# A convolution layer on one core: weight sums and the first image's additions given to transfers

## The chip, the cores and the metric

The kernel runs on one core of one Trainium2 chip. The metric is device time in microseconds (us), the median over several executions. Before the change it is 1605.91 us (three runs, 1605.81 to 1606.45).

## The reference

The input x has 32 images of 256 channels and 28 x 28 points, in float32. Twelve fixed masks (two radius levels, six angle bins, 9 x 9 points) average each channel around each point; a strided 4 x 3 convolution mixes the twelve averages and the 256 channels into 256 channels, and a 1 x 1 convolution of x itself is added. Then comes batch normalization over all images with the batch's own mean and variance, then x is added and negative values are cut off:

```python
xp  = log_pooling(x)                                  # 12 averages of each channel
out = conv(xp, w_conv1, stride (4, 3)) + conv(x, w_center) + b_center
mean, var = out.mean(axis=(0, 2, 3)), out.var(axis=(0, 2, 3))
out = (out - mean) * rsqrt(var + 1e-5) * gamma + beta
return relu(out + x)
```

## The kernel before, in words

The 256 channels stand as 128 partitions times 2 halves (`c` counts input halves, `o` output halves). A step `s` is one input half of one image (s = 2 * image + c); there are 64. In a step VectorE (DVE) makes differences and sums of the columns of x (`differences`), running sums over three and four rows (`three_columns`, `boxes`), and from them three pairs of pooled planes (`first_sum`, `second_sum`, `third_sum`). TensorE (PE) has the first image's products and every other's in the same order: the "middle" products on D1 and D2 (into banks 4 to 7), then the "inner" ones on VD and SD, then the three pairs j = 0, 1, 2 of pooled planes (all into banks 0 to 3).

Each product is made three times, in float32r: the data and the weights are split into a high part (a copy rounded by ScalarE, ACT: lines 397, 400, 418 for data, 392 for weights) and a low part (value minus high part, on DVE: `lo_of_sums`, `lo_of_shifted`, `lo_of_pooled`, and `lo_of_weights`, L557). High x high, low x high and high x low are lines 772 to 774.

The weights are prepared in the first image only, for each input half. `transform_weights` (L523) makes six 256-column combinations of the raw weights on DVE, five instructions at L533 to L543; `split_weights` (L382) and `lo_of_weights` (L547) then split seven groups: group 0 (1536 columns, the combinations, factor 1/4), groups 1 to 4 (256 columns each) and the two outer groups 5 and 6 (512 and 1024 columns). PE waits for group 0 before the middle products, for groups 0 to 4 before the inner ones, and for group 5 and 6 before pairs 0 and 1.

When an image's products have ended, its result is assembled in `y_stage`: ACT copies the middle banks there (`copy_middle`, L433), DVE makes sum and difference of its even and odd columns (`take_middle`, L568 and L571) and adds banks 0 to 3 (`take_y`, L579). ACT then sums it and its squares (`measure`, L451), after finding in the first image a pivot for each channel (`make_pivot`, L442). SyncE (SP) saves y to DRAM (L321). PE may write a bank of the next image only when these readers are done (`m_copied`, `y_ready`).

GpSimd (POOL) issues two adding transfers in each step (L270): `row2` and `ends` get the padded x added from DRAM onto what ACT has put there (`row2_begun`, `ends_begun`). `wait_first` is a wait and a semaphore step on POOL ahead of each. SP loads x and the raw weights; the second part of the first half's weights, the second half of x and all weights of the second half are issued after the first `row2` transfer has landed, in this order. All instructions of an engine's queue run in the order of the program. PE begins with 70 products of zeros (L779), and the tail after the last image reads y and x again, scales, adds, cuts and stores.

The program's own text names the order of the first image (`first_image`, L677) and of every other (`image_steps`, L696). Two lines say what the change turns on:

```python
dve.wait_ge(w_hi_ready, c * len(GROUPS) + g + 1)     # L550, the low part waits for the high one
dve.wait_ge(middle_taken, image + 1 + FREE)          # L576, banks 0-3 are added after the middle
```

Of the kernel before, what the change touches and what calls it, by code (L numbers as in the profile page):

```python
# [7 lines left out]
def conv_bn_relu_program(nc, x, x_wide, w_raw, b_center, gamma, beta, out, y_dram):  # L8
# [62 lines left out]
    with ctx:  # L71
# [61 lines left out]

        def w_part(c, lo, tap):

            if tap < INNER_TAPS:
                return (w_first, w_inner)[c], (lo * INNER_TAPS + tap) * CHANNELS
            return (w_first_outer, w_outer)[c], (lo * (TAPS - INNER_TAPS) + tap - INNER_TAPS) * CHANNELS

# [59 lines left out]
        w_loaded = [[sem(f"w_loaded{c}{part}") for part in range(2)] for c in range(CH)]  # L199
        w_sums_ready = sem("w_sums_ready")  # L200
        w_moved = sem("w_moved")
        w_hi_ready = sem("w_hi_ready")
        w_lo_ready = sem("w_lo_ready")
        zeroed = sem("zeroed")
# [21 lines left out]
        m_copied = sem("m_copied")  # L226
        middle_summed = sem("middle_summed")
# [28 lines left out]
        ZEROED = 7  # L256

        @block.gpsimd
        def _(pool):
            n = 0  # L260
            for edge in (std[:, :], pooled_split[:, 2 * PAIR:2 * PAIR + HALF], row2[:, :], ends[:, :],
                         x_pad[:, 0:2 * H], x_pad[:, X_PAD:X_PAD + 2 * H], x_pad[:, CH * X_PAD:]):
# [26 lines left out]
            with pool.Fori(1, IMAGES) as image:  # L289
                image_sums(image)  # L290
# [9 lines left out]
        def _(sp):  # L300
# [49 lines left out]
            sp.wait_ge(w_lo_ready, CH * len(GROUPS))  # L350
# [30 lines left out]
        def _(act):  # L381
            def split_weights(c, groups):  # L382
                for g in groups:
                    a, b, raw, factor = GROUPS[g]
                    if raw is None:
                        act.wait_ge(w_sums_ready, c + 1)
                        source = view(y_stage, 0, (1, (b - a) * CHANNELS))
# [4 lines left out]
                    nc.scalar.activation(view(dst, at, (1, (b - a) * CHANNELS)), source, ACT.Copy,  # L392
                                         scale=factor).then_inc(w_hi_ready, 1)

# [27 lines left out]
            def copy_middle(image):  # L422
# [7 lines left out]
                if isinstance(image, int) and image == 0:  # L430
                    act.wait_ge(w_lo_ready, CH * len(GROUPS))
# [4 lines left out]

            def make_pivot():

                for o in range(CH):
                    act.wait_ge(y_ready, o + 1 + FREE)  # L440
# [15 lines left out]
            def image_steps(image, first=False, second=False, last=False):  # L456
                for c in range(CH):
                    s = CH * image + c
                    if c == 0 and not first:
                        copy_middle(image - 1)  # L460
                    split_inner(s)
                    if c == 1 and not first:
                        measure(image - 1, 1)
                    if first:
                        split_weights(c, range(len(GROUPS)))
                        act.wait_ge(warmed_up, 1)
                    following = (image, 1) if c == 0 else (image + 1, 0)
# [10 lines left out]
                    if second and c == 0:  # L478
                        make_pivot()
                    if c == 0 and not first:  # L480
# [32 lines left out]
        def _(dve):  # L513
# [9 lines left out]
            def transform_weights(c):  # L523
# [8 lines left out]
                wait_from_one(dve, w_lo_ready, len(GROUPS) * c)  # L532
# [5 lines left out]
                dve.wait_ge(w_moved, 2 * c + 1)  # L538
# [3 lines left out]
                dve.wait_ge(w_moved, 2 * c + 2)  # L542
# [4 lines left out]
            def lo_of_weights(c, groups):  # L547
                for g in groups:
                    a, b, raw, factor = GROUPS[g]
                    dve.wait_ge(w_hi_ready, c * len(GROUPS) + g + 1)  # L550
                    if raw is None:
                        source = view(y_stage, 0, (1, (b - a) * CHANNELS))
# [57 lines left out]
            def differences(image, c):  # L610
# [4 lines left out]
                nc.vector.memset(view(d03, 0, (TALL, 2 * U), (TALL - 1, 2)), 0.0)  # L615
# [23 lines left out]
            def three_columns(image, c):  # L639
# [5 lines left out]
                nc.vector.memset(row3v(-ROW3V_AT, (ROW3V_H, W + 3), (1, EDGES)), 0.0)  # L645
# [31 lines left out]
            def first_image():  # L677

                for c in range(CH):
# [9 lines left out]
                    lo_of_weights(c, [FIRST_OUTER_GROUP - 1])  # L689
# [6 lines left out]
            def image_steps(image, second=False):  # L696
                for c in range(CH):
# [3 lines left out]
                    if c == 0:  # L701
                        take_middle(image - 1)
                    else:
                        lo_of_pooled(s - 1, PAIRS - 1)
# [3 lines left out]
                    if second and c == 0:  # L708
                        take_y(image - 1)
# [12 lines left out]
            dve.sem_inc(middle_taken, FREE)  # L722
# [42 lines left out]
        def _(pe):  # L765
# [17 lines left out]
            with pe.Fori(0, IMAGES) as image:  # L783
                for c in range(CH):
# [29 lines left out]
                    for j in range(PAIRS):  # L814
                        pe.wait_ge(w_lo_ready, c * len(GROUPS) + min(FIRST_OUTER_GROUP + j, len(GROUPS)))
# [55 lines left out]
```

## Time and profile before

| | |
|---|---|
| median of three runs | 1605.91 us (1605.81 to 1606.45) |
| the profiled execution, its own time | 1605.88 us |
| its span, first to last instruction | 1604.1 us |
| PE busy | 1458.2 us (91%) |
| DVE busy | 1474.4 us (92%) |
| ACT busy | 760.6 us (47%) |
| POOL busy | 122.6 us (8%) |
| transfers | 197.55 MB, 123 GB/s over the span |
| mean granted TensorE clock | 0.958 |

Busy shares are averages over the span. The profile's chain of waits gives 86% of the span to PE. A time "idle before" names the engine that ended an engine's idle stretch; a row's start plus its duration is its end, though neighbouring DVE and ACT rows overlap by about 0.1 us, so distances are best taken from start to start.

### The profile page before, as it was taken

To read this page: it belongs to the slowest core of one execution; us is meant where nothing else is said; L and a number is where in the kernel's file an instruction comes from. 1 tells how busy PE (TensorE), PEld (TensorE's weight loads), DVE (VectorE), ACT (ScalarE), POOL (GpSimd) and SP (SyncE) were. 2 spreads that over 40 slices of the span, in tenths; PEclk is the share of its full clock that TensorE was granted. 3 is DMA by queue.
4 is the path that set the end of the run, shared out by engine and by line. 5 is a ranking of instruction groups with operands and counts; after the bars stand their busy time and mean duration, and the time that the engine had idled before them with its cause. 6 is when DMAs were issued, how large, how long until landed. Compare 5 with 4: busy or idle time off the path is not lost.

```text
span 1604.1 us, 22797 instructions
## 1 busy us (share of the span) xinstructions
PE 1458.2 (91%) x8518; PEld 1456.1 (91%) x8518; DVE 1474.4 (92%) x1512; ACT 760.6 (47%) x853; POOL 122.6 (8%) x155
## 2 busy tenths in 40 slices
PE   9899999999999999999999999999999999995000
PEld 9899999999999999999999999999999999995000
DVE  8999999999999999999999999999999999996731
ACT  4345555445444554445444554445444554444632
POOL 1000000000000000000000000000000000000100
PEclk9999999999999999999999999999999999998555
DMA  6244443344333443344333443344334444569999
GB/s 170 69 80 88 84 94 81 80 94 84 81 80 74 85 93 81 80 94 84 81 80 74 87 92 82 80 94 84 83 79 77 87 89 103 155 198 380 419 425 398
DMA packets 46632, 197.55 MB, mean 123 GB/s; under 512 B 5536, under 2 KB 5536, under 8 KB 46624
## 3 DMA queue, kind: packets, MB, share of 16 engines
q0 software_dynamic: 20736, 82.45, 28.4%
q1 hardware_dynamic: 21024, 89.32, 15.2%
q10 hardware_dynamic: 4864, 25.69, 3.9%
q8 instruction: 2, 0.03, 0.0%
q14 instruction: 6, 0.05, 0.0%
HBM read 147.67 MB, written 49.77 MB: 123 GB/s over the span
## 4 chain that ended last, share of the span: by engine, by line
PE 86%; DVE 4%; ACT 4%; ACTq 3%; issue 1%; DMA 0%; DVEq 0%
PE acc L772 29%; PE acc L774 29%; PE acc L773 29%; ACTq L509 3%; ACT phase L506 2%; ACT phase_rest L506 2%; DVE phase_rest L514 1%; DVE pooled_split L515 1%; DVE d L514 0%; DVE inner_split L515 0%; DVE y_stage L514 0%; ACT unread L451 0%; ACT x_pad L506 0%; DMA x_pad<-x 0%; ACT w_inner L392 0%
## 5 line engine op out<-in xcount | busy, mean ns | idle before, releaser
L418 ACT ACTIVATE pooled_split<-phase_rest 128x1456 fp32r<-128x1456 f32 x192 | 273.0, 1422 | 595.5 <-DVE phase_rest L514 595.5
L515 DVE TENSOR_TENSOR pooled_split<-phase_rest,pooled_split 128x1456 fp32r<-128x1456 f32 x192 | 317.8, 1669 | 0.0
L772 PE MATMUL acc<-pooled_split,w_first_outer 128*128 128x364 f32 x768 | 253.8, 330 | 1.1 <-DVE pooled_split L515 1.1
L772 PE MATMUL acc<-pooled_split,w_outer 128*128 128x364 f32 x768 | 252.2, 328 | 1.5 <-DVE pooled_split L515 1.4
L774 PE MATMUL acc<-pooled_split,w_outer 128*128 128x364 f32 x768 | 252.7, 329 | 0.0
L773 PE MATMUL acc<-pooled_split,w_first_outer 128*128 128x364 f32 x768 | 252.5, 329 | 0.0
L773 PE MATMUL acc<-pooled_split,w_outer 128*128 128x364 f32 x768 | 252.5, 329 | 0.0
L774 PE MATMUL acc<-pooled_split,w_first_outer 128*128 128x364 f32 x768 | 252.3, 328 | 0.0
L772 PE MATMUL acc<-inner_split,w_inner 128*128 128x392 f32 (+1 forms) x640 | 215.8, 337 | 2.9 <-DVE w_inner L557 2.9
L772 PE MATMUL acc<-inner_split,w_first 128*128 128x392 f32 (+1 forms) x640 | 216.8, 339 | 0.2 <-DVE inner_split L515 0.2
L773 PE MATMUL acc<-inner_split,w_inner 128*128 128x392 f32 (+1 forms) x640 | 216.6, 338 | 0.0
L774 PE MATMUL acc<-inner_split,w_inner 128*128 128x392 f32 (+1 forms) x640 | 216.6, 338 | 0.0
L774 PE MATMUL acc<-inner_split,w_first 128*128 128x392 f32 (+1 forms) x640 | 215.9, 337 | 0.0
L773 PE MATMUL acc<-inner_split,w_first 128*128 128x392 f32 (+1 forms) x640 | 215.5, 337 | 0.0
L397 ACT ACTIVATE inner_split<-phase_rest 128x1568 fp32r<-128x1568 f32 x64 | 97.2, 1519 | 128.1 <-DVE phase_rest L514 128.1
L772 PEld LDWEIGHTS acc<-pooled_split,w_outer 128*128 128x128 f32 x768 | 144.2, 188 | 2.1 <-DVE pooled_split L515 2.1
L772 PEld LDWEIGHTS acc<-pooled_split,w_first_outer 128*128 128x128 f32 x768 | 144.4, 188 | 1.7 <-DVE pooled_split L515 1.4
L773 PEld LDWEIGHTS acc<-pooled_split,w_outer 128*128 128x128 f32 x768 | 144.5, 188 | 0.0
L773 PEld LDWEIGHTS acc<-pooled_split,w_first_outer 128*128 128x128 f32 x768 | 144.5, 188 | 0.0
L774 PEld LDWEIGHTS acc<-pooled_split,w_outer 128*128 128x128 f32 x768 | 144.4, 188 | 0.0
L774 PEld LDWEIGHTS acc<-pooled_split,w_first_outer 128*128 128x128 f32 x768 | 144.4, 188 | 0.0
L270 POOL DMA_DIRECT2D row<-x_wide x64 | 55.6, 869 | 1093.2 <-ACT row L407 1077.5
(95 smaller groups left out, 2486.1 us busy)
## 6 DMA issues: line engine op xcount, KB each, us to landing
row<-x_wide POOLq DMA_DIRECT2D x64, 558.0 KB, 5.8
ends<-x_wide POOLq DMA_DIRECT2D x64, 504.0 KB, 5.5
x_pad<-x SPq DMA_DIRECT2D x64, 392.0 KB, 3.1
y_dram<-y_stage SPq DMA_DIRECT2D x30, 784.0 KB, 3.3
out<-phase ACTq DMA_DIRECT2D x16, 784.0 KB, 28.4
phase<-y_dram SPq DMA_DIRECT2D x15, 784.0 KB, 16.7
phase_rest<-y_dram SPq DMA_DIRECT2D x14, 784.0 KB, 14.1
out<-phase_rest ACTq DMA_DIRECT2D x14, 784.0 KB, 30.0
```

The costliest lines, as they stand in the source:

```text
L270: return pool.dma_start(view(buf, 0, (1, n_columns * TALL_PITCH)), x_wide[bass.ds(image, 1), :, c, bass.ds((first_column + EDGE) * TALL_PI ...
L397: nc.scalar.activation(view(inner_split, 0, (1, SD)), reused_view(INNER_LOW, (1, SD)), ACT.Copy)\
L418: nc.scalar.activation(view(pooled_split, 2 * j * PAIR, (1, PAIR)), reused_view(POOLED_LOW + 2 * j * PAIR, (1, PAIR)), ACT.Copy)\
L506: nc.scalar.activation(x_slot(d, o), x_slot(d, o), ACT.Relu, bias=bn_shift[:, o:o + 1]).then_inc(relu_done, 1)
L509: act.dma_start(out[tail_image(round_, d)].rearrange("p c w h -> p c (w h)"), x_slot_whole(d)).then_inc(stored[d], 16)
L514: add = lambda out_, a, b: nc.vector.tensor_tensor(out_, a, b, ALU.add)
L515: sub = lambda out_, a, b: nc.vector.tensor_tensor(out_, a, b, ALU.subtract)
L772: nc.tensor.matmul(place, hi_w, hi_in, start=start, stop=False)
L773: nc.tensor.matmul(place, lo_w, hi_in, start=False, stop=False)
L774: return nc.tensor.matmul(place, hi_w, lo_in, start=False, stop=stop)
```

## The change

For the second input half (c = 1) the six weight combinations are no longer made by five DVE instructions. POOL issues a chain of five transfers of 384 KB (128 partitions x 768 columns), one plain and four adding, each waiting until the one before has landed; the three outer terms come from a new array `w_side` laid out on the host by rearranging the raw weights, the middle term is added twice. One DVE instruction makes the other three combinations from the result. The chain stands in POOL's queue between the two transfers of step 0 and those of step 1.

The two outer groups of c = 1 are split without DVE: ACT writes the high part, the scaled weights, and the negated high part in the place of the low one; POOL then adds the scaled weights onto it by a transfer within the core's memory (256 KB and 512 KB). These stand in POOL's queue behind the transfers of step 1.

For image 0, ACT copies the middle banks to `spare` in two forms (as they are, and spread to the other column with sign +1 and -1), later copies banks 0 to 3 straight into `y_stage`, and POOL adds the two forms by two transfers of 784 KB, one after the other, behind the transfers of step 2. DVE has no `take_middle` and no `take_y` for image 0. SP waits for both additions ahead of the steps of image 1, and ACT ahead of the pivot, which moves behind `split_inner` of step 3. Two small memsets of step 0 move from DVE to POOL's opening, and `ZEROED` counts them.

```diff
@@ POOL
                     add_from(image, c, ends, 2, W).then_inc(ends_ready, 16)
+                    if isinstance(image, int) and image == 0:
+                        (sum_weights, low_outer_weights)[c]()
+                    if isinstance(image, int) and image == 1 and c == 0:
+                        add_first_middle()
+            def sum_weights():
+                parts = [w_side[:, k, :] for k in range(3)]
+                parts += 2 * [w_raw[:, 1, RAW_MID:RAW_MID + 3, :].rearrange("p k o -> p (k o)")]
+                pool.dma_start(w_sums(1, 0, 3), parts[0]).then_inc(w_plus_ready, 16)
+                for k in range(1, len(parts)):
+                    wait_first(w_plus_ready, 16 * k)
+                    pool.dma_start(w_sums(1, 0, 3), parts[k], accum_op=ALU.add).then_inc(w_plus_ready, 16)
+            def low_outer_weights():
+                for g in range(INNER_GROUPS, len(GROUPS)):
+                    high, low, whole = outer_weights(g)
+                    wait_first(w_outer_begun, g - INNER_GROUPS + 1)
+                    pool.dma_start(low.bitcast(F32), whole, accum_op=ALU.add).then_inc(w_outer_lo_ready[g - INNER_GROUPS], 16)
+            def add_first_middle():
+                wait_first(y_ready, CH + FREE)
+                wait_first(first_spread, 1)
+                for m in range(2):
+                    if m > 0:
+                        wait_first(first_added, 16 * m)
+                    pool.dma_start(y_stage[:, :], first_middle(m, 0, (1, CH * HW)), accum_op=ALU.add)\
+                        .then_inc(first_added, 16)
@@ SP
             image_steps(0, first=True)
+            sp.wait_ge(first_added, 32)
@@ ACT
+            def begin_outer_weights(g):
+                act.wait_ge(w_loaded[1][1], 16)
+                nc.scalar.activation(high, source, ACT.Copy, scale=factor).then_inc(w_outer_hi_ready, 1)
+                nc.scalar.activation(whole, source, ACT.Copy, scale=factor)
+                act.wait_ge(w_outer_hi_ready, g - INNER_GROUPS + 1)
+                nc.scalar.activation(low, high.bitcast(F32), ACT.Copy, scale=-1.0).then_inc(w_outer_begun, 1)
+            def take_first():
+                for m in range(2):
+                    act.wait_ge(m_copied, m + 1 + FREE)
+                    spread = nc.scalar.activation(first_middle(m, H, ...), first_middle(m, 0, ...), ACT.Copy,
+                                                  scale=(1.0, -1.0)[m])
+                spread.then_inc(first_spread, 1)
+                act.wait_ge(w_lo_ready, ALL_LO)
+                act.wait_ge(pooled_done, PAIRS * CH)
+                for o in range(CH):
+                    nc.scalar.activation(view(y_stage, o * HW, ...), view(acc, 2 * o * BANK, ...), ACT.Copy)\
+                        .then_inc(y_ready, 1)
             def make_pivot():
+                act.wait_ge(first_added, 32)
@@ ACT image_steps
+                    if c == 0 and second:
+                        copy_first_middle()
+                    if first and c == 1:
+                        begin_outer_weights(INNER_GROUPS)
                     split_inner(s)
+                    if c == 0 and second:
+                        take_first()
+                    if c == 1 and second:
+                        make_pivot()
+                        measure(image - 1, 0)
...
+                        split_weights(c, range(len(GROUPS) if c == 0 else INNER_GROUPS))
                         act.wait_ge(warmed_up, 1)
+                    if first and c == 1:
+                        begin_outer_weights(INNER_GROUPS + 1)
@@ DVE transform_weights
+                if c == 1:
+                    dve.wait_ge(w_plus_ready, 5 * 16)
+                    nc.vector.scalar_tensor_tensor(out=w_sums(1, 3, 3), in0=raw(RAW_MID, 3), scalar=-4.0,
+                                                   in1=w_sums(1, 0, 3), op0=ALU.mult, op1=ALU.add)\
+                        .then_inc(w_sums_ready, 1)
+                    return
@@ DVE first_image and image_steps
-                    lo_of_weights(c, range(FIRST_OUTER_GROUP, len(GROUPS)))
+                    if c == 0:
+                        lo_of_weights(c, range(FIRST_OUTER_GROUP, len(GROUPS)))
...
-                    if second and c == 0:
-                        take_y(image - 1)
@@ PE
+                        if c == 0:
+                            pe.wait_ge(w_lo_ready, min(FIRST_OUTER_GROUP + j, len(GROUPS)))
+                        elif j < 2:
+                            pe.wait_ge(w_outer_lo_ready[j], 16)
```

## Rows read from the trace of the kernel before

**Rows 1.** Busy time by stretch: start:end, length, engines' busy us, PEclk, DMA share, GB/s.

```profile
20.00:80.00 60.00, 54.32 (x311) 52.63 (x310) 59.62 (x64) 25.49 (x26) 4.29 (x5) 1.00 0.32 72
80.00:1450.00 1370.00, 1370.00 (x8028) 1369.84 (x8027) 1329.18 (x1342) 662.22 (x739) 104.84 (x121) 1.00 0.42 91
```

**Rows 2.** Timeline of PE, products that began after a wait: start, us, instruction, [idle before].

```profile
41.62 0.44 PE L772 MATMUL acc<-inner_split,w_inner 128*128 128x392 f32 x1 [2.94 <-DVE w_inner L557]
...
53.81 0.43 PE L772 MATMUL acc<-pooled_split,w_outer 128*128 128x364 f32 x1 [1.38 <-DVE pooled_split L515]
...
66.61 0.44 PE L772 MATMUL acc<-inner_split,w_first 128*128 128x392 f32 x1 [0.20 <-DVE inner_split L515]
...
78.49 0.43 PE L772 MATMUL acc<-pooled_split,w_first_outer 128*128 128x364 f32 x1 [1.07 <-DVE pooled_split L515]
```

**Rows 3.** Timeline of DVE, first image, second half.

```profile
37.16 0.96 DVE L543 SCALAR_TENSOR_TENSOR y_stage<-w_stage,y_stage 128x768 f32<-128x768 f32 x1
38.03 1.78 DVE L515 TENSOR_TENSOR inner_split<-phase_rest,inner_split 128x1568 fp32r<-128x1568 f32 x1
39.73 1.75 DVE L557 SCALAR_TENSOR_TENSOR w_inner<-y_stage,w_inner 128x1536 fp32r<-128x1536 f32 x1
...
51.48 0.69 DVE L557 SCALAR_TENSOR_TENSOR w_outer<-w_stage,w_outer 128x512 fp32r<-128x512 f32 x1
...
55.32 1.22 DVE L557 SCALAR_TENSOR_TENSOR w_outer<-w_stage,w_outer 128x1024 fp32r<-128x1024 f32 x1
```

**Rows 4.** Timeline of DVE, second image.

```profile
64.69 1.79 DVE L515 TENSOR_TENSOR inner_split<-phase_rest,inner_split 128x1568 fp32r<-128x1568 f32 x1
...
69.54 1.85 DVE L514 TENSOR_TENSOR y_stage<-acc,y_stage 128x784 f32<-128x784 f32 x2
...
90.69 0.97 DVE L514 TENSOR_TENSOR d<-row,x_pad 128x840 f32<-128x840 f32 x1
```

**Rows 5.** Timeline of ACT.

```profile
29.00 0.85 ACT L407 ACTIVATE ends<-x_pad 128x784 f32<-128x784 f32 x1
35.16 1.52 ACT L397 ACTIVATE inner_split<-phase_rest 128x1568 fp32r<-128x1568 f32 x1 [5.31 <-DVE phase_rest L514]
...
38.15 1.49 ACT L392 ACTIVATE w_inner<-y_stage 128x1536 fp32r<-128x1536 f32 x1 [0.72 <-DVE y_stage L543]
...
62.92 1.53 ACT L397 ACTIVATE inner_split<-phase_rest 128x1568 fp32r<-128x1568 f32 x1 [3.89 <-DVE phase_rest L514]
```

**Rows 6.** Timeline of POOL, the issue of adding transfers.

```profile
6.35 1.23 POOL L270 DMA_DIRECT2D ends<-x_wide  x1
...
30.42 0.86 POOL L270 DMA_DIRECT2D ends<-x_wide  x1 [4.22 <-ACT ends L407]
```

**Rows 7.** Transfers, KB each, us from issue to landing: 0:12, 12:40 (two rows), 1404:1420.

```profile
ends<-x_wide POOLq DMA_DIRECT2D x1, 504.0 KB, 7.7
...
row<-x_wide POOLq DMA_DIRECT2D x1, 558.0 KB, 5.8
ends<-x_wide POOLq DMA_DIRECT2D x1, 504.0 KB, 5.4
...
ends<-x_wide POOLq DMA_DIRECT2D x1, 504.0 KB, 9.6
```

**Rows 8.** Busy time by stretch, as rows 1: while the raw weights load, and after.

```profile
16.00:18.00 2.00, 2.00 (x13) 2.00 (x12) 1.97 (x4) 1.55 (x2) 0.00 (x0) 1.00 1.04 434
...
22.00:24.00 2.00, 2.00 (x13) 2.00 (x13) 2.00 (x3) 1.59 (x2) 0.00 (x0) 1.00 0.03 13
```

**Rows 9.** Busy time by stretch, as rows 1: the granted clock at both ends.

```profile
2.00:4.00 2.00, 2.00 (x8) 2.00 (x7) 0.00 (x0) 0.43 (x2) 1.42 (x5) 1.00 0.97 344
...
1465.00:1466.00 1.00, 0.31 (x2) 0.01 (x1) 0.65 (x1) 0.00 (x0) 0.00 (x0) 1.00 1.02 427
...
1469.00:1470.00 1.00, 0.00 (x0) 0.00 (x0) 0.00 (x0) 0.97 (x3) 0.00 (x0) 1.00 1.00 420
1470.00:1471.00 1.00, 0.00 (x0) 0.00 (x0) 0.27 (x1) 0.70 (x2) 0.00 (x0) 0.54 1.05 439
```

More of the change, by code:

```diff
@@ L138, in w_part, with w_sums, outer_weights, first_middle @@
             return (w_first_outer, w_outer)[c], (lo * (TAPS - INNER_TAPS) + tap - INNER_TAPS) * CHANNELS
+        def w_sums(c, first, n):
+            return view((y_stage, spare)[c], first * CHANNELS, (1, n * CHANNELS))
+        ALL_LO = len(GROUPS) + INNER_GROUPS
+        def outer_weights(g):
+            a, b = (t - INNER_TAPS for t in GROUPS[g][:2])
+            n = (1, (b - a) * CHANNELS)
+            return (view(w_outer, a * CHANNELS, n),
+                    view(w_outer, (TAPS - INNER_TAPS + a) * CHANNELS, n),
+                    view(spare, (6 + a) * CHANNELS, n))
+        def first_middle(m, first, *dims):
+            return view(spare, 12 * CHANNELS + m * CH * HW + first, *dims)
         LAST = IMAGES - 1
@@ L203, in conv_bn_relu_program @@
         w_lo_ready = sem("w_lo_ready")
+        w_outer_hi_ready = sem("w_outer_hi_ready")
+        w_outer_begun = sem("w_outer_begun")
+        w_outer_lo_ready = [sem(f"w_outer_lo_ready{k}") for k in range(2)]
         zeroed = sem("zeroed")
@@ L286, in image_sums @@
                     add_from(image, c, ends, 2, W).then_inc(ends_ready, 16)
+                    if isinstance(image, int) and image == 0:
[22 more added lines that the diff above has]
+                        .then_inc(first_added, 16)
             image_sums(0)
-            with pool.Fori(1, IMAGES) as image:
+            image_sums(1)
+            with pool.Fori(2, IMAGES) as image:
                 image_sums(image)
@@ L349, in _ @@
             image_steps(LAST - 2)
-            sp.wait_ge(w_lo_ready, CH * len(GROUPS))
+            sp.wait_ge(w_lo_ready, ALL_LO)
+            for k in range(2):
+                sp.wait_ge(w_outer_lo_ready[k], 16)
             sp.wait_ge(y_saved, 16 * (LAST - 3))
@@ L458, in image_steps @@
                     s = CH * image + c
-                    if c == 0 and not first:
+                    if c == 0 and second:
+                        copy_first_middle()
+                    elif c == 0 and not first:
                         copy_middle(image - 1)
+                    if first and c == 1:
+                        begin_outer_weights(INNER_GROUPS)
                     split_inner(s)
+                    if c == 0 and second:
[3 more added lines that the diff above has]
+                        measure(image - 1, 0)
                     if c == 1 and not first:
@@ L477, in image_steps @@
                         begin_ends(*following)
-                    if second and c == 0:
-                        make_pivot()
-                    if c == 0 and not first:
+                    if c == 0 and not first and not second:
                         measure(image - 1, 0)
@@ L614, in differences @@
                 wait_from_one(dve, pooled_ready, PAIRS * s)
-                nc.vector.memset(view(d03, 0, (TALL, 2 * U), (TALL - 1, 2)), 0.0)
+                if not (isinstance(image, int) and s == 0):
+                    nc.vector.memset(d_edges(), 0.0)
                 sub(view(d03, 1, (U * TALL, 2), (TALL, U), (1, H)),
@@ L644, in three_columns @@
                 wait_from_one(dve, pooled_done, PAIRS * s - PAIRS + 1)
-                nc.vector.memset(row3v(-ROW3V_AT, (ROW3V_H, W + 3), (1, EDGES)), 0.0)
+                if not (isinstance(image, int) and s == 0):
+                    nc.vector.memset(row3v_edges(), 0.0)
                 dve.wait_ge(inner_lo_ready, 2 * s + 2)
@@ L699, in image_steps @@
                     differences(image, c)
-                    if c == 0:
+                    if c == 1:
+                        lo_of_pooled(s - 1, PAIRS - 1)
+                    elif not second:
                         take_middle(image - 1)
-                    else:
-                        lo_of_pooled(s - 1, PAIRS - 1)
                     lo_of_sums(s)
@@ L845 @@
     w_raw = np.ascontiguousarray(w[:, order][:, :, by_half].reshape(128, halves, len(order), channels))
+    a, c, d, f = (w_raw[:, 1, k] for k in range(4))
+    w_side = np.stack([np.concatenate(part, axis=1) for part in ((d, d, a), (f, a, c), (f, np.zeros_like(a), c))], axis=1)
     def per_partition(v):
```

48 lines of the change are left out of this document (32 added, 16 removed).

## The prediction

> **What bounds the kernel now.** I read the busy time by stretch first, to see which engine is never idle and when. From 80 to 1450 us PE is busy for all 1370 us while DVE has 41 us to spare; from 20 to 80 us it is the other way round, DVE 59.6 of 60 us and PE 54.3 [rows 1]. So after 80 us nothing can be won off PE, and the start is where DVE work holds PE up. The timeline of PE shows the four places: PE had ended at 38.68 and began the second half's products at 41.62; it waited again before 53.81, 66.61 and 78.49, each time for a low part from DVE [rows 2]. The waits sum to 2.94 + 1.38 + 0.20 + 1.07 = 5.6 us. That is the most a change of this start can give. After 78.49 PE runs through to its end, and the tail behind it is released by PE's last products, so what the start gains or loses there is carried to the end unchanged, unless something later holds PE up anew. I therefore follow one number, PE's start of pair 0 of the second image, 78.49 before.
>
> **The chain for the weight sums.** This sets the result, since DVE now stands in its queue before `lo_of_sums(1)` until five transfers have landed. Before, the last instruction of the sums began at 37.16 and PE began 4.46 us later: 0.87 to the low part of the data, 1.70 to the low part of the weights (1536 columns), 1.75 for that and 0.14 to PE [rows 2, 3]; ACT's high part of the sums, 38.15 to 39.64, fits in exactly [rows 5]. The new kernel's one instruction for c = 1 is of the same kind, 768 columns and 0.96 us, and has the same followers. Call its start T. PE begins the second half at 41.62 + (T - 37.16).
>
> T is the landing of the fifth transfer. When does it land?
>
> The first, plain one is issued at 7.6 us, when POOL has ended the issue of `ends` (6.35 + 1.23) [rows 6], but lies in the same queue behind `ends`, which landed at 6.35 + 7.7 = 14.05 [rows 6, 7]. At 434 GB/s its 384 KB need 0.9 us; it shares the engines with SP's loads, which keep them full [rows 8]. I take 2.9 us (bounds 1 and 5): 16.9.
>
> Each of the next four waits for the landing and is then issued. ACT's `ends` copy ended at 29.85 and POOL's issue began at 30.42 [rows 5, 6]: 0.57 us, taken for each. The adding transfers that ran alone took 5.8 us for 558 KB and 5.4 for 504 [rows 7]. Continued to 384 KB by that difference it is 4.5; the upper bound is 5.4 itself; I take 4.65. One beside a deep queue of loads took 9.6 us for 504 KB [rows 7]. The second transfer meets such a queue: SP's loads ended at 22 us [rows 8], will end about 1 us later with the plain one between them, and the second is issued at 17.5. It is neither alone nor beside loads all the way; I take 7.7 us (bounds 4.6 and 9.6), landing 25.2. The three others run alone: 3 x (0.57 + 4.65) = 15.7. T = 40.9. With all low bounds T is 35.3, with all high ones (19, 29.2, then 3 x 5.97) it is 47.
>
> The Trainium skill has a rule that speaks for this edit: its page "DMA: Bandwidth & Descriptors", section "Anatomy of one DMA — SWDGE (gpsimd) path", fits such a transfer at 2.0 us plus its bytes at 436 GB/s, an estimate of 2.9 us for 384 KB. By that rule the chain would be over near 31 us and nobody would wait. This trace disagrees for adding ones: the rule would give 3.3 us for the 558 KB that took 5.8. I go by the row.
>
> So PE begins at 41.62 + 3.74 = 45.4 and stands idle for 6.7 us where it was 2.94.
>
> **The outer groups.** Two DVE instructions go: 0.69 us before pair 0's low part and 1.22 before pair 1's [rows 3], which less the overlap of neighbouring rows is 0.60 and 1.14. ACT makes six copies of 512 or 1024 columns instead; it has room, as it sat idle for 5.31 us before 35.16 [rows 5]. The two transfers are issued behind the chain, `row2` and `ends` of step 1, at about 39 and 48 us, and land by 47 and 54; PE needs them at 57 and 61. Cover about 7 us; nothing. `row2` itself, issued at 25 before, comes at about 37.5 and lands near 44, while DVE, itself 3.7 us late, asks at 47.6. Nothing, but this cover shrinks if T grows no further with it: both sit on the same chain.
>
> **Pair 0, second half.** Its low part is late by 3.74 - 0.60 = 3.1: PE could begin at 56.95. PE's inner products end at 52.43 + 3.74 = 56.2 at full clock. Still a wait of 0.8 us.
>
> **The first image's result.** `take_middle` leaves DVE, but the low part that followed it at 64.69 also needed ACT's high part, which ended at 64.45 [rows 4, 5]: of the 1.9 us removed only 0.24 count. `take_y` before the boxes is 1.85 us [rows 4], 1.77 less the overlap, and counts fully on DVE. By then DVE is late by 3.74 - 0.60 - 1.14 - 0.24 - 1.77 = 0 and its low part of pair 0 is ready at 78.4, as before; PE gets there later than that. So the waits before 66.61 and 78.49 go. PE at full clock: 56.95 + 12.60 (53.81 to 66.41, pairs of image 0) + 10.81 (66.61 to 77.42) = 80.4 against 78.49: +1.9 us. In general this is T - 39.0.
>
> **The clock.** After PE's last product at 1465.3 the granted clock was still 1.00 from 1469 to 1470 and fell within the next microsecond, to half (1.2 GHz), 4.8 us after the work had stopped [rows 9]. The idle stretch of 2.94 us did not bring it down (1.00 over that stretch) [rows 1]. One of 6.7 us will. What it costs: at the start of the program PE's products went 8 in 2 us from 2 to 4 us and 13 later at 2.4 GHz [rows 8, 9]; the lower rate lasted from 1.4 us to nearly 6, some 4.4 us of work, so about 2.2 us are lost (bounds 1 and 3.4). The wait of 0.8 us before pair 0 swallows part: +1.4.
>
> **The two additions to y.** PE ends image 0 at 56.95 + 12.60 + 1.4 = 70.9; ACT copies banks 0 to 3 in some 1.9 us, the time of DVE's two adds from there [rows 4], so the first is issued at 73.4. For 784 KB I continue the rows to 7.4 us each (bounds 6.5 and 8.2 by proportion, twice that if a transfer within the core is slower): landings at 80.8 and 88.8. Queued behind on POOL is `row2` of step 3, which lands near 92.7; DVE used it at 90.69 [rows 4], so DVE is 2.0 us late there. PE's need is later: its first pooled product of that step comes at 78.49 + 12.0 (the three pairs) + 10.8 + 3.3 = 104.6, DVE's low part, about 9 us after the `row2` add (an estimate: in the second image's first half it is the 78.4 less some 67.5 less 1.8), at 101.7. Cover 3 us. ACT waits for the second addition until 88.8, then has six passes over 784 columns for pivot and sums, each about the 0.85 us of its `ends` copy [rows 5] and a short read-out, some 6.2 us; it is free at 95.0 and wanted at about 98. SP's wait delays load and save to 89; the loaded x is wanted past 98. All at nothing; if an addition takes over 1.5 us more than I say, PE pays twice the excess.
>
> The two memsets, of 56 and 124 columns, leave DVE in the first half of image 0, where PE does not wait for DVE: nothing.
>
> **Sum.** +1.9 + 1.4 = +3.3 us. The profiled execution took 1605.88 us, the median 1605.91: 1609.2.
>
> **Rivals.**
> Forecast, chance 0.55: chain late by 3 to 5 us and the clock falls, 1607.5 to 1611.5.
> (B) The chain is late but T is 38 to 40 and the stall, at most 5.8 us, falls between the 2.94 that kept the clock and the 4.8 that lost it, or just over: 1605.91 + (39.2 - 39.0) = 1606.1. For it: the plain transfer and the second may be nearer their low bounds. Against: four adding transfers at over 5 us. Chance 0.22.
> (C) No wait for the chain: it decides if T is under 36.3. Then ACT sets the pace: inner splits 35.16 to 37.4, sums' high part to 38.9, PE at 40.8, pair 0 at 53.81 - 0.8 - 0.6 = 52.4, then 12.60 + 10.81: 75.8, -2.7 us, 1603.2. It needs links of 3.6 us, under every adding transfer in the rows, or a chain unhurt by loads. Chance 0.10. (It is also what follows from the rule of the Trainium skill quoted above.)
> (D) The additions to y come late: a rate within the core half of that from DRAM makes both 14 us, `row2` of step 3 lands 13 us later and PE loses 10 us of it on top: 1619; at a quarter more, 1611. Nothing in the trace shows such a transfer; chance 0.08. The rest, 0.05, is the unforeseen.
>
> **How the numbers follow.** A measurement here tells 0.2% (3.2 us: 1602.7 and 1609.1) from no change. My forecast lies on the upper bound, so its 0.55 is 0.30 slower and 0.25 within; B is 0.19 within and 0.03 slower (the clock falls after all); C 0.07 within and 0.03 faster; D slower; the rest 0.03 slower, 0.02 faster. Together: faster 0.05, within 0.51, slower 0.44. The range takes in B and half of what lies between B and C below, and above a T of 44 with the clock down: 1604.0 to 1612.5.
>
> **What would show it.** PE's wait before the second half's first product: 6.7 us, ended by DVE `w_inner`; DVE idle before its 768-column sum, until 40.9, by a transfer; landings of the chain 5.2 us apart; the granted clock at half for some 4 us from 43 to 50; no wait before 66 and 78. It is wrong if PE's wait is under 4 us, if the clock stays at 1.00, or if PE waits at all between 80 and 110.

## The result, and the profile after

The changed kernel takes 1609.01 us (median of 20 runs, 1607.51 to 1609.81) against 1606.42 us for the kernel before in the same runs (20, 1605.67 to 1607.27): ratio 1.0015, 95% interval 1.0009 to 1.0021, so 2.6 us slower, against a forecast of 1609.2 (3.3 us slower). The profiled execution took 1608.33 us, its span is 1606.6 us.

PE now waits once where it waited four times [rows 2]. The timeline of PE after the change, from 20 to 110 us, has one row with an idle time; the second row here is pair 0 of the second image, the number the prediction followed:

```profile
46.68 0.69 PE L884 MATMUL acc<-inner_split,w_inner 128*128 128x392 f32 x1 [7.77 <-DVE w_inner L665]
...
81.57 0.33 PE L884 MATMUL acc<-pooled_split,w_first_outer 128*128 128x364 f32 x1
```

That pair began at 78.49 before: 3.1 us later. PE's last product is 2.95 us later (1467.94 against 1464.99), the span 2.5. So all of the difference is made before 82 us and carried through.

DVE stands idle ahead of its one sum instruction, and its followers come at the old distances [rows 3]:

```profile
42.21 0.96 DVE L637 SCALAR_TENSOR_TENSOR spare<-w_stage,spare 128x768 f32<-128x768 f32 x1 [6.84 <-DMA spare<-w_raw]
43.09 1.78 DVE L617 TENSOR_TENSOR inner_split<-phase_rest,inner_split 128x1568 fp32r<-128x1568 f32 x1
44.79 1.75 DVE L665 SCALAR_TENSOR_TENSOR w_inner<-spare,w_inner 128x1536 fp32r<-128x1536 f32 x1
```

The chain itself, by POOL's timeline. Each row's start is an issue; the idle time is the wait for the landing before it:

```profile
7.11 1.25 POOL L326 DMA_DIRECT2D spare<-w_side  x1
15.99 0.86 POOL L329 DMA_DIRECT2D spare<-w_side  x1 [7.63 <-DMA spare<-w_side]
25.62 0.86 POOL L329 DMA_DIRECT2D spare<-w_side  x1 [8.77 <-DMA spare<-w_side]
31.19 0.86 POOL L329 DMA_DIRECT2D spare<-w_raw  x1 [4.71 <-DMA spare<-w_side]
37.07 0.86 POOL L329 DMA_DIRECT2D spare<-w_raw  x1 [5.01 <-DMA spare<-w_raw]
```

And the same transfers by their time from issue to landing, asked for one at a time, the first to the fifth:

```profile
spare<-w_side POOLq DMA_DIRECT2D x1, 384.0 KB, 8.3
...
spare<-w_side POOLq DMA_DIRECT2D x1, 384.0 KB, 9.1
...
spare<-w_side POOLq DMA_DIRECT2D x1, 384.0 KB, 5.0
...
spare<-w_raw POOLq DMA_DIRECT2D x1, 384.0 KB, 5.3
...
spare<-w_raw POOLq DMA_DIRECT2D x1, 384.0 KB, 5.1
```

The second ran beside SP's loads, the last three almost alone. A landing and the next issue are 0.5 to 0.6 us apart (15.99 + 9.1 = 25.1, then 25.62).

The granted clock, by stretch (PEclk is the column before the last two): half for the whole stretch in which PE resumed, and full right after.

```profile
46.68:50.46 3.78, 3.78 (x12) 3.78 (x13) 3.75 (x9) 2.08 (x3) 0.87 (x1) 0.50 0.45 83
50.50:52.00 1.50, 1.50 (x11) 1.50 (x9) 1.47 (x2) 0.00 (x0) 0.00 (x0) 1.00 0.99 180
```

By the starts in PE's timeline the products follow each other at 0.32 us at half the clock (49.39, 49.71) and at 0.17 to 0.18 at the full one (51.11, 51.28, 51.46); the 11 of the second row count two products that began before the stretch too.

### The profile page after: what moved, and what is told of

It reads as the page before. It is cut to its first block, busy times and chain, and to the rows that moved or that the text cites. A ratio compares the mean times of both kernels' runs of the same rounds, so it can differ in the third digit from the quotient of the medians.

```text
span 1606.6 us, 22801 instructions
## 1 busy us (share of the span) xinstructions
PE 1459.1 (91%) x8518; PEld 1458.3 (91%) x8518; DVE 1467.5 (91%) x1500; ACT 767.3 (48%) x861; POOL 130.4 (8%) x166
## 4 chain that ended last, share of the span: by engine, by line
PE 88%; ACT 4%; ACTq 3%; DMA 2%; DVE 1%; issue 0%; POOL 0%; POOLq 0%; DVEq 0%
PE acc L884 30%; PE acc L886 29%; PE acc L885 29%; ACTq L611 3%; ACT phase L608 2%; ACT phase_rest L608 2%; DMA spare<-w_side 1%; DMA spare<-w_raw 1%; ACT unread L544 0%; ACT x_pad L608 0%; DMA x_pad<-x 0%; DVE inner_split L617 0%; DVE w_inner L665 0%; DVE y_stage L616 0%; DVE spare L637 0%
```

## The experiments

The profiled programs are named here by what they do; "lost" and "gained" are against the kernel before in the same runs.

**The weight sums back on DVE.**

```diff
-                        (sum_weights, low_outer_weights)[c]()
+                        if c == 1:
+                            low_outer_weights()
...
-                if c == 1:
-                    dve.wait_ge(w_plus_ready, 5 * 16)
...   (the five DVE instructions serve c = 1 again, in spare)
```

> The change without the chain: the second half's weight sums are made by five DVE instructions again, the outer groups and the first image's result stay with transfers. Theory 1 (the chain of five transfers is all of the loss, the other edits gain): PE's wait before the second half falls from 7.77 to about 3 us, the granted clock stays at 1.00, pair 0 of the second image begins near 76.8 instead of 81.57, and the time is 1604.3 us, some 2 us under the kernel before. Theory 2 (the transfers for the outer groups or for y cost as well, by their place in POOL's queue): PE waits somewhere between 50 and 110 us and the time is 1606.5 or more.

Measured: 1604.2 us (before 1606.23; ratio 0.9988, 95% interval 0.9979 to 0.9997; the later results are written the same way). One wait of 2.96 us on PE, pair 0 of the second image at 76.42. Without the chain the change is a gain of 2 us; theory 2 falls. Against expectation the clock did fall, for a wait of the old length, and the wait before pair 0 of the first image was gone. PE arrived later there; in the second execution of this program, below, where the clock stayed up, the wait is back.

**The chain alone**, put into the kernel before.

```diff
                     add_from(image, c, ends, 2, W).then_inc(ends_ready, 16)
+                    if isinstance(image, int) and image == 0 and c == 0:
+                        sum_weights()
...   (transform_weights, w_sums and w_side as in the change)
```

> The kernel before with the chain of five transfers alone. Theory 1: PE's wait is 7.8 us as in the changed kernel, and what DVE no longer gives back (1.74 us of outer groups, 1.9 and 1.77 us of the first image's result) shows as a wait of about 1 us before pair 0 of the second image, which begins at 83.5: 1611.2 us, 4.8 over the kernel before. Theory 2: the chain costs less than that alone, since two of its causes add up only in the changed kernel: 1608 to 1609.

Measured: 1610.65 us (1.0027, 1.0016 to 1.0038), 4.4 lost. PE waits 7.05 and then, as theory 1 has it, before pair 0 of the second image:

```profile
83.05 0.43 PE L794 MATMUL acc<-pooled_split,w_first_outer 128*128 128x364 f32 x1 [1.08 <-DVE pooled_split L531]
```

The interval (1608.8 to 1612.3 us) holds the times of both theories; the wait of 1.08 us before pair 0 is what separates them, and it is there.

**One link fewer, one link more.** Both programs compute wrong weights for the second half: one leaves out an addition of the middle term, the other makes one too many.

```diff
-                parts += 2 * [w_raw[:, 1, RAW_MID:RAW_MID + 3, :].rearrange("p k o -> p (k o)")]
+                parts += 1 * [w_raw[:, 1, RAW_MID:RAW_MID + 3, :].rearrange("p k o -> p (k o)")]   # 3 * in the other
...
-                    dve.wait_ge(w_plus_ready, 5 * 16)
+                    dve.wait_ge(w_plus_ready, 4 * 16)                                              # 6 * 16
```

> The changed kernel with one transfer fewer in the chain (the second addition of the middle term is left out, so the weights of the second half are not the right ones; the work is the same otherwise). Theory 1 (the end of the chain sets PE's start, one for one, and the clock falls only for the long wait): the chain lands at 36.6, PE begins at 41.1 after 2.2 us, clock 1.00, a wait of 0.7 us before pair 0 of the first image: 1603.5 us, 5.5 less than the changed kernel, of which 4.7 are the link and the rest the clock and what hides. Theory 2 (the clock has no part in it): 5.6 - 0.8, so 1604.3 us.

> The changed kernel with one more transfer in the chain (the middle term added a third time, so the weights of the second half are not the right ones). Theory 1: the chain lands at 47.8, PE waits 13.4 us, and as the clock is down already in the changed kernel the step is the link alone, 5.6 us: 1614.6 us. Theory 2 (POOL's queue behind the chain decides too: row2 of step 1 lands near 52.8, DVE wants it at 54.6): nothing more; if it does, over 1616.

Measured: four links 1602.8 us (0.9979, 0.9970 to 0.9988), six links 1615.47 (1.0053, 1.0040 to 1.0067). PE's waits for the second half's weights, four links and then six:

```profile
40.97 0.44 PE L884 MATMUL acc<-inner_split,w_inner 128*128 128x392 f32 x1 [1.89 <-DVE w_inner L665]
52.55 0.43 PE L884 MATMUL acc<-pooled_split,w_outer 128*128 128x364 f32 x1 [0.75 <-DVE pooled_split L617]
```

```profile
51.54 0.69 PE L884 MATMUL acc<-inner_split,w_inner 128*128 128x392 f32 x1 [12.57 <-DVE w_inner L665]
```

Four, five and six links give 1602.8, 1609.0 and 1615.5: 6.2 and 6.5 us a link, where PE's start moved by 5.7 and 4.9. From five to six the end of the chain and PE's start move one for one. From four to five they do not quite: with four links DVE's sum instruction began at 35.83, 6.4 us sooner than with five, and PE's start came 5.14 us behind it instead of 4.47, since the low part of the weights now waited 0.33 us for ACT. At four links the chain has just stopped deciding, and ACT sets the pace, as rival C has it for a T under 36.3:

```profile
35.83 0.96 DVE L637 SCALAR_TENSOR_TENSOR spare<-w_stage,spare 128x768 f32<-128x768 f32 x1 [0.46 <-DMA spare<-w_raw]
```

That the clock has a part is shown by the traces (1.00 throughout with four links, half for 3.8 us of work with five), not by the time: the 1604.3 us of theory 2 lies on the upper bound of the interval for four links. Pair 0 of the second image began at 75.13, 81.57 and 87.53. For six links I had argued that the clock's price was paid already. It was not: the clock was down for 6.2 us of work there, against 3.8.

**The clock held up** by 40 products of zeros while PE waits, and its partner without them. POOL writes the zeros behind the plain transfer of the chain, and ACT waits for the 40 products before it overwrites them with the second outer group.

```diff
-            with pe.Fori(0, IMAGES) as image:
+            def image_products(image):
...
+                    if isinstance(image, int) and image == 0 and c == 1:
+                        pe.wait_ge(idle_zeros, 1)
+                        held = w_outer[:, 2 * CHANNELS:2 * CHANNELS + HALF]
+                        for k in range(40):
+                            idle = nc.tensor.matmul(view(acc, 7 * BANK, (1, HALF)), held[:, 0:P], held, start=False, stop=False)
+                        idle.then_inc(idle_done, 1)
...
+            image_products(0)
+            with pe.Fori(1, IMAGES) as image:
+                image_products(image)
```

> The changed kernel with 40 products of zeros (they add nothing) on PE while it waits for the second half's weights, so that the clock has no idle stretch to fall in; PE's first image stands outside the loop for it. Theory 1 (the fall of the clock took 1.9 us of PE's work, but a wait for pair 0's low part, ready at 58.2, takes its place for the first 1.1 us): PE begins the second half at 46.7 as before, clock 1.00, inner products end at 57.5, a wait of 0.7 us, pair 0 of the second image near 80.9: 0.7 to 0.8 us less than the same kernel without them. Theory 2 (the clock is worth all it took): 1.9 us less. Theory 3 (it is worth nothing, as what is recorded as half is not on the path): the same time.

> The changed kernel with PE's first image outside the loop and no products of zeros, the partner of the run before. Both theories: as the changed kernel, 1609 us, 2.6 over the kernel before, a wait of 7.8 us and a clock that falls to half. If it differs by over 0.5 us, taking the first image out of the loop has a price of its own.

Measured: held 1609.22 us (1.0019, 1.0010 to 1.0028), partner 1609.79 (1.0022, 1.0013 to 1.0031). The mean granted clock of a whole execution was 0.957 to 0.959 in all eleven with the zeros and 0.954 or 0.955 in all eleven without, which speaks for the zeros having held it each time. The medians differ by 0.6 as theory 1 says, but the intervals overlap, so the times alone do not settle it. The timelines, one execution each, say more. With the clock held PE starts the second half at 46.36 at full clock and then waits:

```profile
40.00:46.00 6.00, 6.00 (x35) 5.88 (x34) 4.02 (x3) 2.72 (x5) 0.33 (x1) 1.00 1.03 196
...
46.36 0.45 PE L889 MATMUL acc<-inner_split,w_inner 128*128 128x392 f32 x1 [0.16 <-DVE w_inner L670]
...
58.11 0.40 PE L889 MATMUL acc<-pooled_split,w_outer 128*128 128x364 f32 x1 [0.93 <-DVE pooled_split L622]
...
80.65 0.33 PE L889 MATMUL acc<-pooled_split,w_first_outer 128*128 128x364 f32 x1
```

What the clock takes can be read from the stretch between the start of the second half and pair 0 of the first image. Without its wait the held run needs 10.82 us for it (11.75 - 0.93):

| run | the stretch, us | waiting in it | at half clock | over 10.82: the clock's price |
|---|---|---|---|---|
| clock held | 11.75 | 0.93 | 0 | |
| partner | 12.22 | 0 | 3.4 | 1.40 |
| changed kernel | 12.39 | 0 | 3.8 | 1.57 |
| loads held back (below) | 13.41 | 0 | 6.1 | 2.59 |

So 0.41 to 0.43 of the time at half clock is lost, less than a half, and 0.93 us of that would have been waiting anyway. For the partner that leaves 0.47, and its pair 0 of the second image is indeed 0.43 us later, counted from its own start (34.72 us from 46.17 to 80.89, against 34.29). So in these traces theory 2 falls, and theory 3 too.

The partner was meant to equal the changed kernel. It was 3.4 us over the kernel before where the changed kernel is 2.6, and by what I had set down beforehand a difference of over 0.5 means that taking the first image out of the loop has a price of its own. The intervals overlap, and in its profile pair 0 of the second image and PE's last product come 0.7 us sooner than in the changed kernel; what makes that execution longer lies behind PE's last product. Such a price is neither shown nor excluded, and the held run is compared with its partner alone.

**A chain of three links**, for the outer terms only.

```diff
-                parts += 2 * [w_raw[:, 1, RAW_MID:RAW_MID + 3, :].rearrange("p k o -> p (k o)")]
...
+                    dve.wait_ge(w_plus_ready, 3 * 16)
+                    nc.vector.scalar_tensor_tensor(out=w_sums(1, 3, 3), in0=raw(RAW_MID, 3), scalar=-2.0,
+                                                   in1=w_sums(1, 0, 3), op0=ALU.mult, op1=ALU.add)
+                    nc.vector.scalar_tensor_tensor(out=w_sums(1, 0, 3), in0=raw(RAW_MID, 3), scalar=2.0,
+                                                   in1=w_sums(1, 0, 3), op0=ALU.mult, op1=ALU.add)\
+                        .then_inc(w_sums_ready, 1)
```

> A complete kernel: the change with a chain of three transfers, for the outer terms only; DVE adds twice the middle term and its negative in two instructions instead of one. Theory 1 (the chain costs nothing when it lands before DVE comes for it at 35.3): it lands at 30.7, DVE's second instruction begins at 36.3, ACT's splits set the pace, PE begins the second half at 41.0 after 2.1 us, waits 0.7 before pair 0 and nowhere else: 1602.9 us, 3.4 under the kernel before and as fast as four links. Theory 2 (the transfers cost something by being there, beside the loads): 1604 or more, no better than the change without the chain.

Measured: 1603.13 us (before 1606.38; 0.9979, 0.9970 to 0.9988), 3.3 under the kernel before, and it computes the whole reference. It has the lowest median of the complete kernels here, though its interval overlaps with that of the plain transfer first (1603.53), below. PE's waits:

```profile
40.84 0.44 PE L885 MATMUL acc<-inner_split,w_inner 128*128 128x392 f32 x1 [1.52 <-DVE w_inner L666]
52.42 0.43 PE L885 MATMUL acc<-pooled_split,w_outer 128*128 128x364 f32 x1 [0.74 <-DVE pooled_split L616]
```

PE's start and waits are those of theory 1 (41.0, 2.1 and 0.7); by the time alone the 1604 of theory 2 lies within the interval. DVE's first sum instruction began at 35.15 with no wait for the chain, so a chain over before it is wanted costs nothing that shows.

**The first image's result alone.**

```diff
...   (weight sums as in the first experiment, and also)
-                    if c == 0:
-                        lo_of_weights(c, range(FIRST_OUTER_GROUP, len(GROUPS)))
+                    lo_of_weights(c, range(FIRST_OUTER_GROUP, len(GROUPS)))
...
-                    if first and c == 1:
-                        begin_outer_weights(INNER_GROUPS)
```

> Of the change only the first image's result by ACT and two transfers (and the two memsets); the second half's weight sums and outer groups on DVE as before. Theory 1: the waits of 2.94 and 1.38 us stay, those of 0.20 and 1.07 go: 1605.0 us, 1.3 under the kernel before; the outer groups are then worth the 0.8 us that are left to the run without the chain. Theory 2 (the outer groups gain nothing, their 1.74 us of DVE are cover): 1604.2 us like that run.

Measured: 1604.78 us (0.9988, 0.9979 to 0.9997), a gain of 1.6. The interval holds the times of both theories, the waits decide: those of 2.93 and 1.37 us stay, no other is left, and pair 0 of the second image begins at 77.23. The outer groups add 0.4 to 0.6 us by the medians, within the intervals; in the profiles, 0.8 (76.42), but the clock had fallen in that execution. Against the other execution of that program, with the clock up as here (last experiment, pair 0 at 75.86), it is 1.4 us: 0.6 of it the shorter wait before pair 0 of the first image.

**Loads held back** until the second transfer has landed.

```diff
+            sp.wait_ge(w_plus_ready, 2 * 16)
             load_weights(1, 0)
             load_weights(1, 1)
```

> The changed kernel, but SP issues the two loads of the second half's weights only when the second transfer of the chain has landed. In the changed kernel that second transfer took 9.1 us where the later ones took 5.0 to 5.6. Theory 1 (an adding transfer beside these loads takes about 8 us, whichever it is): the second takes 5.3 us and lands at 21.3, the third 8, the chain lands at 41.5, and the time is 1608.5 us, at most 0.8 under the changed kernel. Theory 2 (what costs is a load queue already deep when the transfer is issued, and one that fills later costs little): the third takes 5.5, the chain lands at 38.9, PE waits 4.5 us: 1605.5 us.

Measured: 1608.75 us (1.0015, 1.0006 to 1.0024). The second and the third transfer, by the time from issue to landing:

```profile
spare<-w_side POOLq DMA_DIRECT2D x1, 384.0 KB, 5.4
...
spare<-w_side POOLq DMA_DIRECT2D x1, 384.0 KB, 8.2
```

Theory 1: the dear transfer is the one beside the loads, whichever it is. The sum instruction began at 41.41, 0.8 sooner; the longer time at half clock (45.87 to 51.93) ate that in the profiled execution.

**The plain transfer first.**

```diff
             assert n == ZEROED
+            pool.dma_start(w_sums(1, 0, 3), w_side[:, 0, :]).then_inc(w_plus_ready, 16)
...
-                pool.dma_start(w_sums(1, 0, 3), parts[0]).then_inc(w_plus_ready, 16)
```

> The changed kernel with the first, plain transfer of the chain issued right behind POOL's memsets, ahead of the two transfers of step 0, instead of behind them; a complete kernel. Theory 1 (the chain's end is its start plus its links): it lands near 8, the second is issued behind ends of step 0 and lands at 17.5, the third meets the loads and takes 9, landing at 27, the chain at 38.3, four less than in the changed kernel; PE waits 4 us and the clock stays up in most executions: 1605.0 us. Theory 2 (the loads of x and of the first weights, which it now meets, are on the path): they land 1 us later, the first products come later than 15.9 and half of it is lost again: 1606.5.

Measured: 1603.53 us (0.9983, 0.9974 to 0.9992), 5.5 less than the changed kernel for one line moved. POOL's timeline, then PE's only wait from 20 to 110 us, then the stretch behind it:

```profile
3.57 0.68 POOL L298 DMA_DIRECT2D spare<-w_side  x1
...
7.75 0.86 POOL L329 DMA_DIRECT2D spare<-w_side  x1 [0.26 <-issue]
16.77 0.85 POOL L329 DMA_DIRECT2D spare<-w_side  x1 [8.16 <-DMA spare<-w_side]
26.30 0.86 POOL L329 DMA_DIRECT2D spare<-w_raw  x1 [8.69 <-DMA spare<-w_side]
...
41.78 0.69 PE L884 MATMUL acc<-inner_split,w_inner 128*128 128x392 f32 x1 [2.32 <-DVE w_inner L665]
...
41.78:45.12 3.34, 3.34 (x10) 3.34 (x11) 3.31 (x9) 2.08 (x3) 0.67 (x1) 0.50 0.50 92
```

The sum instruction began at 37.32, 4.9 sooner. Its first product came at 16.75 in the profiled execution, later than 16.05 in the changed kernel; at the start PE's products reached the full rate about 2 us later in it (between 7 and 9 us, not 5 and 7), so I do not charge the transfer with it. Theory 2 falls by the time. My 1605.0 was 1.5 too high, and I had the clock staying up: in this profiled execution it was down to half when PE resumed after a wait of only 2.32 us, and stayed there until 45.1. It is the shortest wait here with which it fell.

**The sums on DVE, executed again.**

> The same program as the one with the weight sums on DVE, one more execution. There the granted clock fell to half from 42.6 to 46.0 us for a wait of 2.96 us, which in the kernel before (2.94) and with the first image's result alone (2.93) left it at 1.00. Theory 1 (whether so short a wait is noticed differs from execution to execution): the clock may stay at 1.00 here with the same wait. Theory 2 (it belongs to the program): it falls again at the same place.

Measured: one execution, 1602.92 us. The same stretch in the two executions of the one program, first the earlier, then this one:

```profile
42.00:44.00 2.00, 2.00 (x10) 2.00 (x9) 2.00 (x7) 1.78 (x2) 0.00 (x0) 0.65 0.03 8
44.00:46.00 2.00, 2.00 (x8) 2.00 (x7) 1.97 (x3) 0.00 (x0) 0.86 (x1) 0.50 0.21 33
```

```profile
42.00:44.00 2.00, 2.00 (x13) 2.00 (x12) 2.00 (x7) 1.79 (x2) 0.00 (x0) 1.00 0.03 8
44.00:46.00 2.00, 2.00 (x13) 2.00 (x12) 1.97 (x3) 0.00 (x0) 0.86 (x1) 1.00 0.21 33
```

Theory 1: the wait was 2.96 us in one and 2.85 in the other, and the clock fell in one only. That the difference of 0.11 us does not decide it is borne out by the kernel before (2.94) and the first image's result alone (2.93), where it stayed up, and by the plain transfer first (2.32), where it fell. Pair 0 of the second image began at 76.42 and at 75.86; the wait of 0.76 us before pair 0 of the first image was back in the second.

## Why the prediction was right

The forecast was 1609.2 us by +1.9 for the chain and +1.4 for the clock; measured 1609.0. The mechanism was right: a late chain sets PE's start, the clock falls in the wait, nothing else holds PE up. That the number fits to 0.2 us is luck, twice over. The kernel before took 1606.42 us in these runs and not the 1605.91 that I started from, and the change cost 2.6 us and not 3.3. And the 3.3 was itself made of errors that cancel: PE's start was 1.3 us later than in the working, what came between it and pair 0 of the second image 1.5 us shorter (under "The sum" below). Step by step:

*The chain sets PE's start.* Shown by five and six links, by the chain alone and by its removal. T was given as 40.9 and was 42.2. Terms were off in opposite directions: the plain transfer landed at 15.4 (7.11 + 8.3), not 16.9; the second took 9.1 us, not 7.7, which cancels it; the later ones with their gaps took 5.6 to 5.9, not 5.22, and that is the 1.3 us. The distance from T to PE's start was 4.46 in the working and 4.47 in the trace.

*The rule of the Trainium skill* ("DMA: Bandwidth & Descriptors", section "Anatomy of one DMA — SWDGE (gpsimd) path") gives an estimate of 2.9 us for 384 KB. The adding transfers took 5.0 to 5.3 nearly alone and 9.1 beside loads. The measurement decides: rival C, which the rule supported, needed links of 3.6 us.

*The clock falls in the long wait.* It did, and PE worked 3.8 us at the lower level, which cost 1.6 us by the table above, instead of the 2.2 I had from 4.4 us and a full half. The claim used to get there, that a wait of 2.94 us leaves the clock up, was drawn from one execution and is not a rule: 2.96 us went with a fall in another program, and 2.32 in a third. So the condition of rival B, a wait short enough to keep the clock up, is not one that a length of wait guarantees. Whether the clock falls in some executions of the kernel before, its one profile does not show.

*What swallows a part of it.* I had 0.8 us of waiting before pair 0; the run with the clock held shows 0.93. So the clock's net part was 1.6 - 0.9 = 0.6 us, not 1.4.

*Outer groups, at nothing.* Right: no wait of PE for their transfers. They stood longer in the queue than I said: the 256 KB one, issued at 38.68, landed after 12.4 us at 51.1, as `row2`, `ends` and it were all issued within 2 us of the last link; PE wanted it at 59.07. `row2` of step 1 landed at 37.60 + 9.5 = 47.1 and DVE used it at 48.96, a cover of 1.9 us instead of 3.6.

*`take_middle` 0.24 us, `take_y` 1.77.* DVE's wait for ACT before the low part of step 2 is there (1.58 us), and PE waits nowhere after 59. The first image's result alone gained 1.6 us.

*The additions to y, at nothing.* Rival D falls. They were quicker than the 7.4 us I took from reads of DRAM:

```profile
y_stage<-spare POOLq DMA_DIRECT2D x1, 784.0 KB, 5.9
...
y_stage<-spare POOLq DMA_DIRECT2D x1, 784.0 KB, 6.8
```

*The sum.* Pair 0 of the second image was given as 78.49 + 3.3 = 81.8 and began at 81.57. Counted from PE's start (45.4 given, 46.68 measured) the way there was 1.5 us shorter than in the working: 12.39 us to pair 0 of the first image instead of 12.99, 11.97 for the three pairs instead of 12.60, and 10.53 for the inner products of image 1 instead of 10.81. The last two terms, 0.9 us together, were mis-sized: I had taken them from the kernel before as work at full clock, with only the shown waits taken off, but in that trace the product at 58.18 began 0.43 us after the one before it, where the rest follow at 0.17 to 0.18, with no idle time shown, and at each shown wait another 0.2 to 0.3 us are lost beside it (78.49 - 77.08 = 1.41, of which 1.07 are shown, and the next product only at 78.76). PE was held up in these stretches by more than the idle times say. Of PE's 2.95 us the tail gave back 0.4; where in the tail, I have not traced. From the start of PE's last product to the end of the span the thirteen profiled executions need 138.7 to 140.2 us, whatever their start was, so 0.4 is within what this part varies by.

## What to carry to other kernels

A chain of dependent adding transfers costs its links' full latency, here 5.3 to 5.9 us from issue to issue for 384 KB and 8.7 to 9.6 beside loads, so count the links and place the end of the chain before the time the consumer comes: three links with one more vector instruction beat five links with one less by 5.9 us, and issuing the plain link 3.5 us earlier, ahead of the two transfers of step 0, ended the chain 4.9 us sooner and was worth 5.5. A change that bundles several moves can lose by one of them; undo each alone before dropping the lot. And before pricing a fallen clock at what the engine lost, look for the wait that it hides; and before taking a stretch as work at full speed, look at the distances between its products.

## What the runs showed of the hardware

The granted clock is not a function of the program alone, and the length of a wait does not decide it either. It stayed at 1.00 with waits of 1.52, 1.89, 2.85, 2.93 and 2.94 us, and fell to half, for 3.3 and 3.4 us of work, with waits of 2.32 and 2.96; one and the same program is on both lists (2.85 and 2.96). With the 2.96 it fell only 0.9 us after PE had resumed (41.70, then 42.6). After the waits of 6.4 us and more the work began at half clock each time and stayed there for 3.4, 3.8, 5.1, 6.1 and 6.2 us.

A stretch at half clock cost less than half of itself: 1.4 us for 3.4, 1.6 for 3.8, 2.6 for 6.1, 2.7 for 6.2, since the products followed at 0.32 us and at 0.17 to 0.18 otherwise. That is a spread of 1.3 us between programs. How much of the 2.3 us between the fastest and the slowest run of the changed kernel is the clock's is not shown; the tail alone varies by 1.5 us between the profiled executions.

An adding transfer within the core's memory took 5.9 and 6.8 us for 784 KB. One from DRAM took, nearly alone, 5.0 to 5.3 for 384 KB in the changed kernel and 5.4 to 5.8 for 504 to 558 KB [rows 7]. Whether the larger size is carried quicker within the core is not shown, as no transfer of 784 KB from DRAM was run.
